# Attention with VectorE's sums two units behind its maxima, and denominators as four 32-column products

## The reference

```
x = x + attn(layernorm(x))      # qkv = h @ W_qkv; score = q k^T / 8, causal mask; softmax; @ v; @ W_out
x = x + ffn(layernorm(x))       # h @ (W + up_aux @ lora_up @ lora_down @ down_aux)^T + b
```

## Time and profile before

| | us |
|---|---|
| median of 3 runs | 1910.45 (1909.38 to 1913.12) |
| profiled execution | 1910.15, span 1908.1 |
| TensorE busy | 1833.8 (96%), granted clock 0.991 of full |
| VectorE busy | 1272.3 (67%) |
| ScalarE busy | 806.7 (42%) |
| GpSimd busy | 972.8 (51%) |

### The profile page before, as it was taken

How to read it: one execution, slowest core, us unless ns; L and a number is a source line. 1 busy time by engine, 2 the same in 40 slices (tenths; PEclk the granted TensorE clock), 3 DMA queues, 4 the chain that set the end, 5 groups by cost and what they waited for, 6 DMA issues and landing times. The chain is left out here.

```text
span 1908.1 us, 34290 instructions
## 1 busy us (share of the span) xinstructions
PE 1833.8 (96%) x13464; PEld 1128.0 (59%) x13464; DVE 1272.3 (67%) x2123; ACT 806.7 (42%) x982; POOL 972.8 (51%) x532
## 2 busy tenths in 40 slices
PE   7999998999999999999999999999999999998998
PEld 5877776555555555555555555555555555554897
DVE  5364652868676767676776767686777676747565
ACT  3222123454545454545454454545454545454221
POOL 1011000666675858575665666666758585746211
PEclk9999998999999999999999999999999999998999
DMA  5646445212121212222121312121212121023551
GB/s 204 223 179 232 164 157 210 68 35 78 41 73 46 72 46 68 62 58 67 46 74 51 80 45 79 40 74 46 67 46 73 46 68 51 24 73 102 177 192 56
DMA packets 150782, 171.33 MB, mean 90 GB/s; under 512 B 44618, under 2 KB 91744, under 8 KB 150624
## 3 DMA queue, kind: packets, MB, share of 16 engines
q1 hardware_dynamic: 150624, 169.15, 28.0%
HBM read 97.02 MB, written 71.57 MB: 88 GB/s over the span
## 5 line engine op out<-in xcount | busy, mean ns | idle before, releaser
L1017 DVE TENSOR_REDUCE f_part_max<-b_ring 128x1 f32<-128x512 f32 (+3 forms) x1200 | 675.3, 604 | 317.5 <-PE b_ring L850 213.5
L948 ACT ACTIVATE b_probs<-b_scores 128x1024 f32<-128x1024 f32 (+3 forms) x640 | 567.4, 898 | 615.5 <-PE b_scores L822 357.9
L1123 POOL TENSOR_TENSOR b_sum_pool<-b_sum_pool,b_probs 128x1024 f32<-128x1024 f32 x237 | 569.2, 2402 | 32.1 <-POOL b_sum_pool L1123 0.5
L1123 POOL TENSOR_TENSOR b_sum_pool<-b_probs 128x1024 f32<-128x1024 f32 x48 | 115.7, 2411 | 324.8 <-DVE g_sum_dve L1049 308.7
L822 PE MATMUL b_scores<-f_split 64*128 64x512 f32 (+2 forms) x1920 | 269.5, 383 | 9.1 <-ACT b_probs L948 7.3
L822 PE MATMUL b_scores<-b_split 64*128 64x512 f32 (+2 forms) x1920 | 268.0, 381 | 3.3 <-ACT b_probs L948 3.1
L886 PE MATMUL b_o_acc<-b_probs,f_v_in 128*64 128x512 f32 (+3 forms) x1280 | 270.5, 544 | 0.0
L886 PE MATMUL b_o_acc<-b_probs,b_v_in 128*64 128x512 f32 (+3 forms) x1280 | 269.0, 541 | 0.7 <-ACT b_probs L948 0.7
L1049 DVE TENSOR_TENSOR g_sum_dve<-g_sum_dve,b_probs 128x768 f32<-128x768 f32 (+3 forms) x243 | 229.5, 944 | 34.1 <-ACT b_probs L948 26.1
L822 PEld LDWEIGHTS b_scores<-b_split 64*128 64x128 f32 x1920 | 165.6, 185 | 51.0 <-issue 20.4
L822 PEld LDWEIGHTS b_scores<-f_split 64*128 64x128 f32 x1920 | 168.2, 187 | 46.0 <-issue 19.4
(11 more groups left out here) (135 smaller groups left out, 2288.5 us busy)
## 6 DMA issues: line engine op xcount, KB each, us to landing
f_raw<-k_t SPq DMA_DIRECT2D x32, 512.0 KB, 4.8
f_raw<-q_t SPq DMA_DIRECT2D x32, 512.0 KB, 5.6
g_recip<-r_t SPq DMA_DIRECT2D x128, 128.0 KB, 3.0
o_t<-g_o_norm SPq DMA_DIRECT2D x64, 256.0 KB, 2.0
q_t<-a_stage_a SPq DMA_DIRECT2D x32, 256.0 KB, 2.4
q_t<-a_stage_d SPq DMA_DIRECT2D x32, 256.0 KB, 2.0
k_t<-a_stage_a SPq DMA_DIRECT2D x32, 256.0 KB, 2.0
k_t<-a_stage_d SPq DMA_DIRECT2D x32, 256.0 KB, 2.0
```

Of the source, the lines that this page charges most:

```text
L948: nc.scalar.activation(probs[s % PR][:, :, off:], scores[s % 2][:, :, off:], ACT.Exp, scale=scale).then_inc(exp_done, 1)
L1017: nc.vector.tensor_reduce(part_max[:, h, ib, c:c + 1], rowwise[h][:, 0:width], AX.X, ALU.max).then_inc(chunk_reduced, 1)
L1123: nc.gpsimd.tensor_tensor(sum_pool[:], first, probs[s % PR][:], ALU.add).then_inc(pool_added, 1)
```

## The change

The sums of VectorE run two slots behind its chunk reductions (`SUM_LAG = 2`, `units_summed_at`); in the last item VectorE first catches up and then adds each unit in its own slot. Everything that follows a tile's sums moves by two slots, one pair: the ones products on TensorE, ScalarE's copy, the reciprocals, POOL's normalise. SP's order is unchanged. The denominators are made by four products of 32 columns and 256 queries instead of two of 64 columns and 512; each lands in 32 of the 128 partitions. The copy of them is 256 wide instead of 512, and the spread takes four transfers of 64 partitions instead of two of 128. The last tile's denominators in `project_and_ffn` change in the same way.

```
+    SUM_LAG = 2
...
-            if s in starts:
-                uses.append(("denom", (starts[s] - 1) % TI))
+            if s - SUM_LAG in starts:
+                uses.append(("denom", (starts[s - SUM_LAG] - 1) % TI))
...
+    def units_summed_at(n, s):
+        if n == LAST_ITEM:
+            return [(n - 1, U - SUM_LAG + i) for i in range(SUM_LAG) if s == 0] + [(n, s)]
+        if s >= SUM_LAG:
+            return [(n, s - SUM_LAG)]
+        return [(n - 1, U + s - SUM_LAG)] if n else []
...
                 def invert(n, t):
-                    for h in range(2):
-                        sp.dma_start(den_spread[:, h, :], den_row[h * D:h * D + 1, :].rearrange(
+                    for c in range(4):
+                        h, half = divmod(c, 2)
+                        sp.dma_start(den_spread[half * D:(half + 1) * D, h, :], den_row[c * P // 4:c * P // 4 + 1, :].rearrange(
                             "o (p i) -> o p i", i=NB)).then_inc(den_moved, 16)
...
                 def denominators(n, t, now, before):
-                    for h in range(2):
-                        last = nc.tensor.matmul(denom[head(h), :], consts["ones"][:, 0:D],
-                                                sum_dve[t % 2][:, h, :], start=True, stop=True)
+                    for c in range(4):
+                        h, half = divmod(c, 2)
+                        cols = slice(half * DEN, (half + 1) * DEN)
+                        last = nc.tensor.matmul(denom[c * P // 4:(c + 1) * P // 4, 0:DEN], consts["ones"][:, 0:P // 4],
+                                                sum_dve[t % 2][:, h, cols], start=True, stop=True)
...
-                        for late in late_tile(n, s, previous):
+                        for late in late_tile(n, s - SUM_LAG, previous):
                             denominators(*late, n, ring_before[following]["denom", late[1]])
...
-                        for late in late_tile(n, s - 3, previous):
+                        for late in late_tile(n, s - 3 - SUM_LAG, previous):
                             copy_denominators(*late)
...
-                        if dve_adds(n, s):
-                            add_unit(n, s)
-                        for late in late_tile(n, s - 5, previous):
+                        for unit in units_summed_at(n, s):
+                            if dve_adds(*unit):
+                                add_unit(*unit)
+                        for late in late_tile(n, s - 5 - SUM_LAG, previous):
                             reciprocals(*late)
...
-                        for late in late_tile(n, s - (10 if following else 6), previous):
+                        for late in late_tile(n, s - SUM_LAG - (10 if following else 6), previous):
                             normalise(*late)
```

More of the change, by code:

```diff
@@ L31 @@
 STAGES = 3
+DEN = TILE // 2
 LOADS = 2
@@ L974, in copy_denominators @@
                     act.wait_ge(denom_made, n * TI + t + 1)
-                    act.wait_ge(den_moved, (n * TI + t) * 32 + 1)
-                    denom = ring[:, ring_banks["denom", t][0], :]
+                    act.wait_ge(den_moved, (n * TI + t) * 64 + 1)
+                    denom = ring[:, ring_banks["denom", t][0], 0:DEN]
                     nc.scalar.copy(den_row[:], denom).then_inc(den_copied, 1)
@@ L1072, in reciprocals @@
                 def reciprocals(n, t):
-                    dve.wait_ge(den_moved, (n * TI + t + 1) * 32 + 1)
+                    dve.wait_ge(den_moved, (n * TI + t + 1) * 64 + 1)
                     nc.vector.reciprocal(recip_spread[:], den_spread[:]).then_inc(inverted, 1)
@@ L1210, in project_and_ffn @@
         last_t = tiles // 2 - 1
-        last_denom = y[1][:, 0:2, :].rearrange("p n c -> p (n c)")
+        last_denom = y[1][:, 0, 0:DEN]
         with nc.Block() as block:
@@ L1248, in finish_last_o @@
                     sp.wait_ge(tail["den_copied"], o_tiles + 1)
-                    for h in range(2):
-                        sp.dma_start(tail["den_spread"][:, h, :], tail["den_row"][h * P // 2:h * P // 2 + 1, :].rearrange(
-                            "o (p i) -> o p i", i=NB)).then_inc(tail["den_moved"], 16)
+                    for c in range(4):
+                        h, half = divmod(c, 2)
+                        sp.dma_start(tail["den_spread"][half * P // 2:(half + 1) * P // 2, h, :],
+                                     tail["den_row"][c * P // 4:c * P // 4 + 1, :].rearrange("o (p i) -> o p i", i=NB)
+                                     ).then_inc(tail["den_moved"], 16)
                     sp.wait_ge(tail["inverted"], o_tiles)
@@ L1338, in _ @@
                 pe.wait_ge(tail["dve_added"], tail["dve_ops"])
[L1339 to L1342, removed]
+                for c in range(4):
+                    h, half = divmod(c, 2)
+                    cols = slice(half * DEN, (half + 1) * DEN)
+                    last = nc.tensor.matmul(last_denom[c * P // 4:(c + 1) * P // 4, :], consts["ones"][:, 0:P // 4],
+                                            tail["sum_dve"][last_t % 2][:, h, cols], start=True, stop=True)
                 last.then_inc(tail["denom_made"], 1)
@@ L1378, in _ @@
                 act.wait_ge(tail["denom_made"], o_tiles)
-                act.wait_ge(tail["den_moved"], (o_tiles - 1) * 32 + 1)
+                act.wait_ge(tail["den_moved"], (o_tiles - 1) * 64 + 1)
                 nc.scalar.copy(tail["den_row"][:], last_denom).then_inc(tail["den_copied"], 1)
@@ L1448, in _ @@
                 norm(0, 0, 1)
-                dve.wait_ge(tail["den_moved"], o_tiles * 32 + 1)
+                dve.wait_ge(tail["den_moved"], o_tiles * 64 + 1)
                 nc.vector.reciprocal(tail["recip_spread"][:], tail["den_spread"][:]).then_inc(tail["inverted"], 1)
@@ L1515, in attend @@
                 "recip": sb("recip", [P, TILE]),
-                "den_row": sb("den_row", [P, TILE]),
+                "den_row": sb("den_row", [P, DEN]),
                 "den_spread": sb("den_spread", [P, 2, NB]),
```

## The result

The changed kernel takes 2024.1 us (median of four runs, 2018.5 to 2032.7) beside 1910.5 us for the kernel before on the same chip: ratio 1.0596, 95% interval 1.0552 to 1.064, slower. The prediction was 1980, with a range of 1912 to 2015. The direction and the waits came as forecast, and the time lies 9 us above the range. The profiled execution took 2027.9 us, with a span of 2026.0.

What follows compares the result with a forecast made beforehand. TensorE was taken as the bound. Per item, gains of 1.6 + 1.4 against 7.45 us of waits net +4.45; fifteen items give 66 after a 0.9 deduction, the last item 4: 1910.15+66+4 = 1980 us, range 1912 to 2015.

Steps and rivals of the forecast that it cites:

- The bound: Whole kernel: TensorE, busy 1833.8 of 1908.1 us, sets the time; other engines count only where it waits for them.
- Denominators: Ones products on TensorE: 0.65 us per tile instead of 1.03, saving 22 us over 63 tiles (0 to 32).
- Rival 4: The 32-column products do not run side by side at all; about 2025 us, chance 0.04.
- A: Tile 1 to 2: TensorE waits for VectorE's burst (1.4 us) and its wait for the reciprocal's spread (0.9); 2.3 us.
- B: Last pair of tile 2: TensorE waits because tile 1's reciprocals come late behind POOL's normalise and the spread; 2.1 us.
- C: Tile 2 to 3: TensorE waits for VectorE's burst between two chunks, with no reciprocal in it; 1.4 us.
- D: Next item's first scores: POOL starts tile 3 later, so the maxima are placed late and TensorE waits; 1.65 us.
- The sum of the four: Per item, TensorE's four new waits together: 2.3+2.1+1.4+1.65 = 7.45 us.
- The last item: It has no chunks; ScalarE already waits for POOL and the SP chain starts one pair later: +4 us (0 to 8).

Runs made afterwards that it cites:

- e2: The changed kernel without the lag of the sums (SUM_LAG = 0), so only the four 32-column products and four spread transfers; 1895.2 us.
- e4: The changed kernel with POOL normalising two units sooner, at the slot of the kernel before, in all items but the last; 1981.7 us.
- e3: The changed kernel with SP placing the next item's maxima before it stores the o of tile 2; 1995.3 us.
- e6: The changed kernel with the edits of e3 and e4, and the spread in two transfers of two rows each; 1952.7 us.
- e8: The changed kernel with VectorE adding each unit in its own slot; only what follows the sums stays one pair later; 1917.2 us.
- e5: The changed kernel with TensorE computing four score units of each item twice, those right before its four waits; 2016.0 us.
- e7: e2 with the spread in two transfers of two rows each instead of four; 1894.8 us.
- e9: e2 with VectorE adding POOL's partial sum after the last diagonal unit instead of the second; 1900.7 us.
- e1: The changed kernel with the old two 64-column products and two spreads per tile, so only the sums and what follows run late; 2003.8 us.
- e10: The changed kernel with VectorE adding POOL's partial sum after the last diagonal unit instead of the second; 2066.4 us.

## Why the prediction was wrong in size and right in kind

- **The bound.** Right: TensorE was the bound and its waits decide. All the added idle time is in the chunk waits and the placing. An item grew from 90.0 to 97.6 us, where I had 94.
- **Denominators, minus 22 us (21 in the sum: 1.4 in each of fifteen items).** Right in the length, somewhat high in the worth. 252 products of 593 ns were busy for 64.9 us together; the 504 new ones for 40.3, 0.64 us per tile where I took 0.65:

```profile
L910 PE MATMUL b_ring<-g_sum_dve,p_ones 128*32 128x256 f32 x504 | 40.3, 391 | 0.0
```

  That is 24.6 us less, but each group overlaps its neighbours on TensorE, and e2's busy time fell by 16.7 us and its total by 15. Rival 4 falls: eight products of 0.39 us each pass in 0.64, so the column groups do run side by side. That its time of about 2025 us is near the measured one is chance. The new products do not reach half of the old 1.03 us, though. The Trainium skill ("TensorE: Matmul & The Clock Gate", Measured speedup vs the span model) has three products of 32 columns 2.38 times as fast as one after another; the prediction's estimate from it was near 0.5 for four, and the trace has 0.64. Whether a switch of tiling mode takes the rest, no run here isolates.
- **A, 2.3 us.** Place and both parts right, too low: 2.80 on average over the 15 items, 1.48 to 3.51. The first item, with no reciprocal before it, has the 1.48 of the burst alone. In nine items VectorE waits 1.84 to 2.05 us for the spread, where I took 0.9. In the other five it waits 0.15 at most, and an add of 1024 columns takes 1.82 to 2.13 us instead of 1.22.
- **B, 2.1 us.** Right in mechanism (e4), 1.46 on average, but spread from nothing to 4.04. In the five items whose A had no fall of the clock behind it, B is 2.06 to 4.04, 2.87 on average; in the ten whose A had one, it is 0 to 1.75.
- **C, 1.4 us.** 1.97 on average, 1.67 to 2.81. It is near 1.68 in nine items, 0.3 more than I had. In the others VectorE's adds take longer beside GpSimd; I had taken their times from rows where they did not.
- **D, 1.65 us.** 1.16 on average, but 1.90 in the eight items where TensorE ran at full clock before it. e3 confirms the chain.
- **The sum of the four.** 7.45 us per item predicted, 111.1/15 = 7.4 measured. Less the 23.9 us of old waits that is 87.2; mine was 7.45 x 15 - 0.9 - 23.9 = 86.9. That they agree so closely is partly luck: A and C came out larger than I had them, and so would B and D at full clock, but the slower clock ate into both.
- **The last item, plus 4 us.** Not seen as idle time: TensorE's waits in it sum to 4.2 us before and 4.8 after. They changed their kind, from VectorE's sums (2.49 us) to ScalarE's exponentials (2.19, 0.70 and 1.86), and two falls of the clock stand at them, which the kernel before has not.
- **What failed** is the sum "Fifteen items give 67 ... 1910.15+66+4 = 1980 us". It prices each wait at its own length and lets TensorE come back at full clock. I read "its granted clock is near full" from the kernel before, whose waits reach 0.94 us, and carried it over to a kernel with waits of 1.5 to 4. The missing term is about 49 us (55.7 by the sum of windows). With it, with the products at 16.7 us instead of 21 (4.3 more), 0.7 us more idle time than my 86.9, no 4 us for the last item, and the 2.3 us outside the window, the sum is 1980 + 49.2 + 4.3 + 0.7 - 4 - 2.3 = 2027.9, the time of the profiled execution. It closes because the terms are differences of the same rows; what it shows is that the clock's term alone is larger than the 9 us by which the range was missed, and that the rest nearly cancels.

How sure is it that the waits bring the clock down? 29 of the 33 falls lie at them. Every run that took waits away has fewer falls (e3, e4, e6, e8), filling them with work did the same (e5), and the kernels whose waits are small have at most one fall at such a wait (before, e2, e7, e9). The length of a wait matters. Over the chunk and placing waits of all twelve traces, the number with a fall in them or within 2 us behind them:

| length of the wait, us | waits | with a fall |
|---|---|---|
| 0.3 to 1.5 | 284 | 0 |
| 1.5 to 2 | 136 | 50 |
| 2 to 3 | 72 | 38 |
| 3 and more | 60 | 53 |

So e1, with 118.5 us idle but no wait over 2.6, loses 27.5, and e3, with 114.2 idle and eleven waits of 3 and more, loses 45.4; and e10 has 28 falls, fewer than the changed kernel, but more long ones, and loses as much (64.9). Open is which single wait does it: 3.30 us passed without a fall and 1.68 had one. No run here sorts that out.

## What to carry to other kernels

When a change puts waits of 1.5 us and more into TensorE where it was busy throughout, price each wait twice: its length, and a fall of the clock at it in some of the cases (here at 29 of the 43 waits of 1.5 us and more, some 1.6 us lost for each fall, about half as much again on top of the new idle time; the slowed engine then waits less at the next place). Of two runs here with about the same idle time, the one with the longer waits lost more to the clock. A queue that is worked through strictly in order turns a small delay into a late transfer for everything behind it: a sum that nobody waits for was two units late, and the maxima, GpSimd's tile, the normalise, the spread and the next item's placing came late with it. And take a change with two halves apart before judging it: here one half gains 0.7% and the other costs 5%.

## What the runs showed of the hardware that was not expected

- TensorE's clock falls from 2.4 to 1.2 GHz for 3.4 us, now and then 6.8, at waits of 1.7 to 4 us, 29 times in the changed kernel, and in 22 of these the fall comes after work has begun again (1057.40 and 1058.00 above).
- Some VectorE operations beside GpSimd's adds or normalise take far longer: an add of 768 columns 2.06 us for 0.95 (above). The copy of 1024 columns that opens a tile takes 0.68 us with GpSimd idle and 2.28 beside its last add and normalise; both are of the changed kernel:

```profile
1058.35 0.68 DVE L1053 COPY g_sum_dve<-b_probs 128x1024 f32<-128x1024 f32 x1
...
1094.16 2.28 DVE L1053 COPY g_sum_dve<-b_probs 128x1024 f32<-128x1024 f32 x1
```

- What SP pays to issue these transfers goes by their number, not their size: four rows of 1 KB take 2.40 us, 0.60 each, and two of 2 KB took 1.14, 0.57 each. The 2.05 us for two in the same rows is an outlier; in 60 of the 64 tiles of the kernel before the two took 1.1 to 1.2.
